# Router steps of a pair moved two pairs on, with norms, low parts, context loads and expert choices reordered around them

## The chip, the cores and the metric

The kernel runs on one core of a Trainium2 chip. The metric is the device time of one launch in microseconds (us), taken as the median of a few runs. The engines are called PE (TensorE), DVE (VectorE), ACT (ScalarE), POOL (GpSimd) and SP (SyncE, which here only issues DMAs). Each runs its own list of instructions in order and waits on semaphores for the others.

## What is computed

Sixteen batches of 128 rows of width 256 go through cross attention with 16 heads and then through a feed-forward layer with one shared expert and twelve routed experts, of which each row takes its best two:

```
x = x + attention(layernorm(x), ctx, ctx, masks)          # 16 heads of 16
n = layernorm(x)
logits = (n @ Wr + br) / 1.5                               # 12 experts
top_val, top_idx = top_k(logits, 2);  w = softmax(top_val)
x = x + geglu(n @ Ws1 + bs1) @ Ws2 + bs2 + sum_k w_k * expert[top_idx_k](n)
```

All matrix products keep about fp32 accuracy: an operand is split into a high part and a low part (fp32r), and three products are added up.

## The kernel before

**Stages.** The first third of the time is attention, worked in eight pairs of batches (PAIRS = 8, two batches each, pair p holds batches 2p and 2p+1). Then the rows are scattered by expert into a DRAM table by indirect DMAs on POOL (`scatter`, L1913), half of the shared expert is computed meanwhile, and 43 tiles of 128 rows go through the routed experts (from about 263 us to the end, matmuls L790 and L823). At the end the rows are gathered back.

**One pair on PE** (`pair`, L664; the order is written out by hand). PE works on three things interleaved: the attention of pair p, the projections of the next pair (steps "k", "q", "v", called by `put`), and the transposes of the normalised x of the pair after it (step "xT"). For a batch it computes the scores of all 16 heads into the four banks of ps_s (`scores`, L563: a mask product, L568, then 24 matmuls, L574), transposes the probabilities in four groups (`prob_transposes`, L585), multiplies them by the values (`values`, L595) and transposes the result (`out_transposes`, L603). The scores of a batch can be written only when DVE has taken those of the batch before.

**DVE in a pair** (`pair`, L1451). The scores of a batch are two units: unit 4p and 4p+1 for batch 2p, 4p+2 and 4p+3 for batch 2p+1. Each takes a `softmax_max` (L1317) and a `softmax_add` (L1324), and ACT then takes the exponential in place. `softmax_add` of a unit waits until PE has transposed the two groups of the unit two before it, since they share a buffer. Between them DVE makes the low parts of k, q and xT, the statistics of the first layer norm (`ln1_stats`, L1218), the division by the softmax sum (`norm`, L1334), the residual with the statistics of the second layer norm (`residual`, L1344), and xn2p, the second layer norm of a finished pair (`ln2_apply`, L1359).

**The router** of a pair has two steps: "r" transposes xn2p on PE (L488), ACT copies it out (xn2T, L997), and "l" multiplies by Wr (L539), DVE adds the bias into logits (L1283). In pair p the kernel before makes the router of pair p-1, near the end of the pair, directly behind `ln2_apply(p-1)`.

**Banks.** The steps of all pairs share two PSUM banks in turn. `order(p)` (L314) lists the steps of a pair, `base_of(p)` (L324) is the number of its first one, and a step's number decides its bank. The semaphore xb_free counts the steps whose bank is free again; step n on PE waits until step n-2 is free.

**Choices.** When the logits of batches 0 to 7 are there, DVE picks the best two experts (`choose(0, 0)`, `choose(1, 0)`, L1406), PE counts the ranks (step "n", in pair 6), and `row_numbers(0)` (L1428) makes the table rows and releases rows_ready, which POOL waits for before its first scatter. Batches 8 to 11 and 12 to 15 follow later in the same way.

**POOL in a pair** (the loop under `normalise_x(2)`): the first norm of pair p+2 (`normalise_x`, L1843), the scale of the second norm of pair p-1 (`rstd`, L1798), the split of the context of pair p+2 (`split_ctx`, L1833), and a share of the conversion of the shared expert's weights. **SP in a pair** (L429): load the context, save xn2p, zero an eighth of the scatter table (`fill`, L415, 3.3 MB each, eight of them). All eight fills must have landed before the first scatter.

Of the kernel before, what the change touches and what calls it, by code (L numbers as in the profile page):

```python
# [18 lines left out]
B, S, D = 16, 128, 256  # L19
# [33 lines left out]
def build(nc, x_d, ctx_d, pad_d, sub_d, wq_d, wk_d, wv_d, bias_d, bst_d, tab_d, ws1_d, ws2_d, w1_d,  # L53
# [260 lines left out]
    def order(p, first, last):  # L314

        if last:
            return ["r", "l", "n"]
        if first:
            return ["xT", "k", "q", "v", "xT"]
        if isinstance(p, int) and p == PAIRS - 2:  # L320
            return ["k", "q", "n", "v", "r", "l"]
        return ["k", "q", "v", "xT", "r", "l"]

    def base_of(p, first):  # L324

        return len(FIRST) if first else 6 * p + len(FIRST) - 1
# [15 lines left out]
    def each_pair(eng, body):  # L342

        body(0, 0, True, False)
        with eng.Fori(0, (PAIRS - 4) // 2) as i:
            body(i * 2 + 1, 1, False, False)
            body(i * 2 + 2, 0, False, False)
        body(PAIRS - 3, 1, False, False)
# [25 lines left out]
    with block:  # L374
# [3 lines left out]
        def _(sp):  # L378
# [61 lines left out]
            sp.wait_ge(c_split, PAIRS - 1)  # L440
            load_ctx(PAIRS - 1)
# [41 lines left out]
        def _(pe):  # L483
# [180 lines left out]
            def pair(p, par, first, last):  # L664
# [5 lines left out]
                def put(s, parts=(0, 1), again=False):  # L670
# [6 lines left out]
                    elif s in ("r", "l"):  # L677
                        router(s, p - 1, idx, bank, index_of("r", p, first, last) + 1)
# [17 lines left out]
                else:  # L696
                    prev = p * 2 - 1
                    prob_transposes(prev, 0)
                    put("k", (0,))
                    prob_transposes(prev, 1)  # L700
# [11 lines left out]
                    put("n")  # L712
# [238 lines left out]
        def _(sc):  # L951
# [82 lines left out]
            def pair(p, par, first, last):  # L1034
# [5 lines left out]
                def put(s, again=False):  # L1040
# [4 lines left out]
                    if s == "r":  # L1045
                        router(s, idx, bank)
# [9 lines left out]
                else:  # L1056
                    prev = p * 2 - 1
                    prob_copy(prev, 0)
# [4 lines left out]
                    exp(p * 4, 0)  # L1063
                    out_copy(prev)
                    put("q")
# [6 lines left out]
                put("xT", first)  # L1072
                prob_copy(cur, 3)
                put("r")
# [4 lines left out]
                exp(p * 4 + 3, 3)  # L1079

# [127 lines left out]
        def _(ve):  # L1208
# [242 lines left out]
            def pair(p, par, first, last):  # L1451
# [5 lines left out]
                def put(s, again=False):  # L1457
# [6 lines left out]
                    elif s in ("r", "l"):  # L1464
                        router(s, p - 1, idx, bank)
# [13 lines left out]
                else:  # L1479
# [606 lines left out]
```

## Time and profile before

| | us |
|---|---|
| median of 3 runs (643.98 to 647.44) | 644.26 |
| profiled execution, its own time | 646.02 |
| its span | 644.2 |
| PE busy / DVE / POOL / ACT | 582.1 / 447.1 / 364.5 / 282.6 |

PE is busy for 90% of the span. The chain of work that ended last runs for 72% of the span over PE, 12% over DVE and 5% over POOL. In the line of the page that shows PE's granted clock in 40 slices of 16 us, the last two thirds are at nine tenths or more throughout, while the attention stage goes up and down:

```profile
PEclk9799879789799989799999999999999999999998
```

### The profile page before, as it was taken

What the parts mean: (1) busy time and instruction counts of PE and PEld (TensorE: products, weight loads), DVE (VectorE), ACT (ScalarE), POOL (GpSimd) and SP (SyncE); (2) the same over time, 40 slices, a digit from 0 to 9 for tenths busy, and PEclk for the clock granted to TensorE, in tenths of its full rate; (3) what the DMA queues carried; (4) which work ended last, traced back from release to release, by engine and by line L of the source; (5) the groups of instructions that cost most, each with busy time, mean ns of one, the idle gap of its engine ahead of it and who ended that gap; (6) DMA issues with size and microseconds to landing.
All of it is one profiled execution on the core that took longest, in us unless ns stands there. A gap on an engine that the chain in (4) does not pass through costs nothing.

```text
span 644.2 us, 14068 instructions
## 1 busy us (share of the span) xinstructions
PE 582.1 (90%) x4092; PEld 479.8 (74%) x4093; DVE 447.1 (69%) x976; ACT 282.6 (44%) x629; POOL 364.5 (57%) x419
## 2 busy tenths in 40 slices
PE   7597979879788778799999999999999999999995
PEld 6465757656556777587887888878887888889995
DVE  5588668577678867667766677766676776665767
ACT  3255536454356623344444444444444444444432
POOL 3533151452108878699983886778886684000773
PEclk9799879789799989799999999999999999999998
DMA  9940651628651432364535365263465241110443
GB/s 289 395 173 31 216 185 61 244 99 292 227 214 68 172 140 91 122 225 156 204 136 179 95 222 188 81 228 130 144 222 183 86 131 33 33 34 18 139 134 121
DMA packets 47620, 98.91 MB, mean 154 GB/s; under 512 B 4449, under 2 KB 23521, under 8 KB 47585
## 3 DMA queue, kind: packets, MB, share of 16 engines
q1 hardware_dynamic: 36192, 50.41, 22.5%
q0 software_dynamic: 10976, 47.72, 22.2%
q10 hardware_dynamic: 416, 0.33, 0.2%
q8 instruction: 21, 0.34, 0.2%
q14 instruction: 15, 0.11, 0.1%
HBM read 57.15 MB, written 39.19 MB: 150 GB/s over the span
## 4 chain that ended last, share of the span: by engine, by line
PE 72%; DVE 12%; issue 5%; POOL 5%; ACT 3%; SPq 2%; DMA 1%; DVEq 0%; ACTq 0%; POOLq 0%
PE ps_s L790 29%; PE ps_o L823 9%; PE ps_o L824 5%; PE ps_s L752 4%; PE ps_t L800 3%; PE ps_t L585 3%; PE ps_s L568 2%; POOL rows_in L1913 2%; PE ps_s L574 2%; DVE prob L1324 2%; PE ps_x L510 2%; PE ps_t L510 2%; DVE nmax L1317 1%; PE ps_s L800 1%; PE ps_x L539 1%
## 5 line engine op out<-in xcount | busy, mean ns | idle before, releaser
L790 PE MATMUL ps_s<-ring,xTh 128*128 (+1 forms) x516 | 153.4, 419 | 0.5 <-DVE xTl L1638 0.5
L790 PEld LDWEIGHTS ps_s<-ring,xTh 128*128 128x128 f32 x516 | 89.2, 191 | 14.6 <-DVE xTl L1638 0.8
L1624 DVE TENSOR_TENSOR ag<-ps_s,up_bias 128x512 f32<-128x512 f32 x129 | 89.1, 691 | 12.1 <-PE ps_s L790 7.4
L823 PE MATMUL ps_o<-ring,hTh 128*128 x258 | 96.0, 410 | 0.8 <-issue 0.8
L1814 POOL TENSOR_TENSOR ring<-stage,ring 128x512 fp32r<-128x512 f32 x76 | 95.7, 1292 | 1.1
L790 PE MATMUL ps_s<-ring,xTl 128*128 (+1 forms) x258 | 81.0, 395 | 0.0
L824 PE MATMUL ps_o<-ring,hTl 128*128 x258 | 72.3, 280 | 0.0
L1800 POOL TENSOR_TENSOR ve<-mv,eps 128x2 f32<-128x2 f32 x16 | 3.5, 216 | 116.9 <-DVE mv L1356 100.6
L2025 POOL DMA_INDIRECT gath<-rows_out,idx_out x32 | 31.0, 968 | 65.8 <-DMA rows_out<-y_row 56.3
L1629 DVE TENSOR_TENSOR ag<-ag,ps_s 128x256 f32<-128x256 f32 x129 | 54.3, 421 | 16.0 <-ACT ps_s L1105 0.5
L1105 ACT ACTIVATE ps_s<-ag 128x256 f32<-128x256 f32 x129 | 50.2, 389 | 32.4 <-DVE ag L1624 31.0
L980 ACT ACTIVATE probT<-ps_t 128x512 f32<-128x512 f32 x64 | 37.8, 597 | 52.4 <-PE ps_t L585 51.2
L790 PEld LDWEIGHTS ps_s<-ring,xTl 128*128 128x128 f32 x258 | 48.8, 189 | 11.4
L1113 ACT ACTIVATE hTh<-ps_t 128x256 fp32r<-128x256 f32 x86 | 33.1, 385 | 53.6 <-PE ps_t L800 53.6
L1647 DVE TENSOR_TENSOR y_row<-ps_o,y_lo 128x256 f32<-128x256 f32 x43 | 18.3, 425 | 55.0 <-ACT y_lo L1128 55.0
L823 PEld LDWEIGHTS ps_o<-ring,hTh 128*128 128x128 f32 x258 | 48.5, 188 | 10.6 <-issue 1.0
L1827 POOL TENSOR_TENSOR ring<-stage,ring 128x512 fp32r<-128x512 f32 x40 | 51.0, 1300 | 1.2
L1633 DVE TENSOR_TENSOR hTl<-ps_t,hTh 128x256 fp32r<-128x256 f32 x86 | 36.1, 420 | 21.5 <-issue 16.8
L824 PEld LDWEIGHTS ps_o<-ring,hTl 128*128 128x128 f32 x258 | 48.9, 189 | 0.0
L1324 DVE TENSOR_TENSOR prob<-ps_s,nmax 128x1024 f32<-128x1024 f32 x32 | 39.1, 1221 | 13.2 <-PE ps_t L585 12.9
L752 PE MATMUL ps_s<-xgh,ring 128*128 128x256 f32 x256 | 47.4, 292 | 0.3
L1317 DVE TENSOR_REDUCE nmax<-ps_s 128x8 f32<-128x1024 f32 x32 | 38.9, 1217 | 10.3 <-PE ps_s L574 8.7
(254 smaller groups left out, 1290.1 us busy)
## 6 DMA issues: line engine op xcount, KB each, us to landing
rows_in<-y_row SPq DMA_DIRECT2D x8, 3328.0 KB, 13.7
stage<-in_w POOLq DMA_DIRECT2D x12, 1536.0 KB
stage<-in_w POOLq DMA_DIRECT2D x12, 768.0 KB, 5.4
up_bias<-in_bias POOLq DMA_DIRECT2D x12, 768.0 KB, 5.1
xrow<-rows_in SPq DMA_DIRECT2D x43, 128.0 KB, 2.2
rows_out<-y_row SPq DMA_DIRECT2D x43, 128.0 KB, 1.8
c_raw<-in_ctx SPq DMA_DIRECT2D x8, 256.0 KB, 10.7
xn_all<-xn2p SPq DMA_DIRECT2D x8, 256.0 KB, 2.6
```

Of the source, the lines that this page charges most:

```text
L752: last = pe_.matmul(ps_s[:, c, half * D:(half + 1) * D], weights(place, off + k * 2 * HS + half * D + col, P), x[:, k, :], start=n == 0, s ...
L790: last = pe_.matmul(ps_s[:, i, :], x[:, c, :], weights(place, off + c * 2 * HR + i * 2 * D, 2 * D), start=n == 0, stop=n == 5)
L823: pe_.matmul(ps_o[:, :], hTh[i][:, c, :], weights(place, a, 2 * D), start=i == 0 and c == 0, stop=False)
L824: pe_.matmul(ps_o[:, 0:D], hTl[i][:, c, :], weights(place, a, D), start=False, stop=False)
L980: act.activation(probT[:, g, :, :], ps_t[:, bank, :].rearrange("p (j t) -> p j t", j=4), ACT.Identity).then_inc(pt_copied, 1)
L1105: act.activation(ps_s[:, i, D:2 * D], ag[i][:, 1, :], ACT.Gelu).then_inc(gelu_done[i], 1)
L1317: vec.tensor_reduce(nmax[:, :, :], group_scores(n), AX.X, ALU.max, negate=True).then_inc(maxed, 1)
L1324: vec.tensor_tensor(prob[n % 2][:, :, :, :].rearrange("p a j t -> p j a t"), src, nmax[:, :, :].rearrange("p j (a o) -> p j a o", o=1).bro ...
L1624: vec.tensor_tensor(ag[i][:, :, :].rearrange("p a n -> p (a n)"), ps_s[:, i, :], bias, ALU.add)\
L1629: vec.tensor_tensor(ag[i][:, 0, :], ag[i][:, 0, :], ps_s[:, i, D:2 * D], ALU.mult).then_inc(hid_done[i], 1)
L1814: last = pool.tensor_tensor(lo_ap[:, c:c + PIECE], src[:, c:c + PIECE], hi_ap[:, c:c + PIECE].bitcast(f32), ALU.subtract)
L1827: last = pool.tensor_tensor(both[:, c:c + 2, 1, :], raw[:, c:c + 2, :], both[:, c:c + 2, 0, :].bitcast(f32), ALU.subtract)
```

## The change

The steps are reordered; the arithmetic stays the same.

- **PE.** In pairs 2 to 6 the router is that of pair p-2, whose xn2p was made in the pair before, and it stands at the beginning: "r" first of all, "l" behind the first half of "k". Pair 6 makes the router of pair 5 as well, at its end ("R" and "L"), with three filler matmuls (`spin`) between them. Step "xT" moves behind the third group of values, and the rank step "n" in pair 6 moves from the middle to behind `out_transposes(cur)`. Pairs 0 and 1 make no router.
- **ACT.** "q" is copied before `out_copy(prev)`, "xT" after `out_copy(cur)`.
- **DVE.** "l" goes ahead of the first `softmax_add`, "k" ahead of the second; `ln1_stats` is for pair p+2 in place of p+3; `ln2_apply` moves behind `softmax_add(4p+3)`, "xT" after it. `choose(0, 0)` moves from pair 5 to pair 6, `choose(1, 0)` from the end of pair 5 to the middle of pair 6, "n" and `row_numbers(0)` to behind `ln2_apply`.
- **POOL.** `split_ctx` comes first, `normalise_x` and `rstd` last, and then a new wait for xn2_ready, that is until DVE has made xn2p.
- **SP.** xn2p is saved first, then the context is loaded (for pair p+3), then the table is filled.

```
--- before.py
+++ after.py
         if isinstance(p, int) and p == PAIRS - 2:
-            return ["k", "q", "n", "v", "r", "l"]
-        return ["k", "q", "v", "xT", "r", "l"]
+            return ["r", "l", "k", "q", "v", "n", "R", "L"]
+        return ["r", "l", "k", "q", "v", "xT"]
...
             def pair(p, first):
-                sp.wait_ge(c_split, p + 2)
-                load_ctx(p + 2)
-                if not first:
+                if first:
+                    sp.wait_ge(c_split, 2)
+                    load_ctx(2)
+                    fill(1)
+                    sp.wait_ge(c_split, 3)
+                    load_ctx(3)
+                else:
                     save_xn2(p - 1)
-                fill(p + 1)
+                    sp.wait_ge(c_split, p + 3)
+                    load_ctx(p + 3)
+                    fill(p + 1)
...   (PE)
                     prev = p * 2 - 1
+                    put("r")
                     prob_transposes(prev, 0)
                     put("k", (0,))
+                    put("l")
                     prob_transposes(prev, 1)
...
                     out_transposes(prev)
-                    put("n")
...
                 values(0, par, cur, (1,))
-                put("xT", again=first)
                 prob_transposes(cur, 3)
                 values(0, par, cur, (2,))
-                put("r")
+                put("xT", again=first)
                 values(0, par, cur, (3,))
-                put("l")
                 out_transposes(cur)
+                put("n")
                 next_scores()
+                if "R" in todo:
+                    put("R")
+                    pe.wait_ge(xb_free, index_of("L", p, first, last) - 1)
+                    spin(3, step_bank[bank_of("L", p, first, last)][:, 0:D])
+                    put("L")
...   (DVE)
                 else:
+                    put("l")
                     softmax_add(p * 4, 0)
-                    softmax_shift(p * 4 + 1, 1, p * 2)
+                    softmax_max(p * 4 + 1, 1, p * 2)
                     put("k")
-                    if isinstance(p, int) and p == PAIRS - 3:
+                    softmax_add(p * 4 + 1, 1)
...
+                    if isinstance(p, int) and p == PAIRS - 2:
                         choose(0, 0)
-                    elif not isinstance(p, int):
-                        ln1_stats(p + 3)
+                    else:
+                        ln1_stats(p + 2)
+                    put("q")
                     softmax_max(p * 4 + 2, 2, p * 2 + 1)
                     norm(p - 1, 1)
-                    put("q")
+                if isinstance(p, int) and p == PAIRS - 2:
+                    choose(1, 0)
                 softmax_add(p * 4 + 2, 2)
                 if not first:
                     residual(p - 1, 1)
+                softmax_max(p * 4 + 3, 3, p * 2 + 1)
+                softmax_add(p * 4 + 3, 3)
+                if not first:
+                    ln2_apply(p - 1)
+                put("xT", first)
                 if isinstance(p, int) and p == PAIRS - 2:
                     put("n")
                     ve.wait_ge(xb_free, index_of("n", p, first, last) + 1)
                     row_numbers(0)
-                softmax_max(p * 4 + 3, 3, p * 2 + 1)
-                if not first:
-                    ln2_apply(p - 1)
-                softmax_add(p * 4 + 3, 3)
-                put("xT", first)
                 norm(p, 0)
                 residual(p, 0)
-                if first:
-                    ve.wait_ge(x_rest_in, 16)
-                    ve.wait_ge(router_in, 32)
-                    ln1_stats(3)
-                put("l")
                 softmax_max(p * 4 + 4, 0, p * 2 + 2)
-                if isinstance(p, int) and p == PAIRS - 3:
-                    choose(1, 0)
+                put("L")
...   (POOL)
             for p in range(1, PAIRS - 1):
                 if p + 2 < PAIRS:
-                    normalise_x(p + 2)
-                rstd(ln2_var, ln2_rs, mv2, ve2, rs2, p - 1, pstep2)
-                if p + 2 < PAIRS:
                     split_ctx(p + 2)
...
+                if p + 2 < PAIRS:
+                    normalise_x(p + 2)
+                rstd(ln2_var, ln2_rs, mv2, ve2, rs2, p - 1, pstep2)
+                gp.wait_ge(xn2_ready, p)
```

## Rows read from the trace of the kernel before

**Rows 1.** Windows by pair (pairs 1, 2, 6): window, length, busy times, PE clock, DMA.

```profile
44.10:69.89 25.79, 22.36 (x223) 16.43 (x219) 18.80 (x38) 12.90 (x20) 11.77 (x16) 0.87 0.28 101
69.89:95.88 25.99, 22.55 (x223) 16.54 (x219) 18.15 (x33) 12.90 (x20) 8.55 (x10) 0.89 0.44 156
...
174.74:199.45 24.71, 20.16 (x226) 14.84 (x223) 18.31 (x41) 12.39 (x19) 5.26 (x7) 0.99 0.56 207
```

**Rows 2.** Windows within pair 2, the long first part and the end.

```profile
69.89:85.50 15.61, 15.58 (x170) 11.65 (x166) 12.89 (x24) 9.63 (x16) 1.09 (x3) 1.00 0.27 89
85.50:95.88 10.38, 6.97 (x54) 4.89 (x53) 5.26 (x10) 3.26 (x5) 7.47 (x8) 0.72 0.71 258
```

**Rows 3.** Timeline of PE, end of pair 2: start, duration, engine, line, [idle before].

```profile
87.56 0.63 PE L488 MATMUL ps_t<-const,xn2p 128*128 128x128 f32 x4 [2.06 <-DVE xn2p L1364]
...
89.89 1.82 PE L539 MATMUL ps_x<-wr,xn2T 128*128 128x12 f32 x8 [1.35 <-ACT xn2T L997]
```

**Rows 4.** Timeline of PE, end of pair 6.

```profile
192.60 0.70 PE L585 MATMUL ps_t<-const,prob 128*128 128x128 f32 x4 [1.70 <-ACT probT L980]
...
194.77 0.63 PE L488 MATMUL ps_t<-const,xn2p 128*128 128x128 f32 x4 [1.12 <-DVE xn2p L1364]
...
196.09 1.06 PE L539 MATMUL ps_x<-wr,xn2T 128*128 128x12 f32 x8 [0.33 <-ACT xn2T L997]
197.00 0.64 PE L603 MATMUL ps_o<-const,outT 128*128 128x128 f32 x4
```

**Rows 5.** Windows, the same work in pair 6 and in pair 2.

```profile
194.77:199.45 4.68, 4.31 (x52) 2.99 (x53) 2.60 (x7) 2.98 (x4) 3.46 (x5) 1.00 0.42 153
87.56:95.88 8.32, 6.97 (x53) 4.86 (x53) 3.20 (x8) 2.97 (x4) 5.49 (x6) 0.65 0.88 320
```

**Rows 6.** Timeline of PE, pair 2 and the end of pair 0.

```profile
71.31 0.66 PE L585 MATMUL ps_t<-const,prob 128*128 128x128 f32 x4
...
77.51 1.04 PE L568 MATMUL ps_s<-mask_b,ident_b 128*128 x4
...
79.39 0.66 PE L603 MATMUL ps_o<-const,outT 128*128 128x128 f32 x4
...
84.50 0.64 PE L585 MATMUL ps_t<-const,prob 128*128 128x128 f32 x4
```

```profile
41.74 0.66 PE L603 MATMUL ps_o<-const,outT 128*128 128x128 f32 x4 [0.78 <-ACT outT L985]
```

**Rows 7.** Timeline of ACT, the copy of xn2T in pair 2.

```profile
89.24 0.60 ACT L997 ACTIVATE xn2T<-ps_t 128x512 f32<-128x512 f32 x1 [3.45 <-DVE xTl L1268]
```

**Rows 8.** Window of DVE in pair 2: length, busy, PE clock; and its low part of k.

```profile
75.88:85.40 9.52, 9.17 (x20) 1.00 0.01 2
```

```profile
77.02 1.40 DVE L1275 SCALAR_TENSOR_TENSOR km_lo<-ps_t,const,km_hi 128x512 fp32r<-128x512 f32 x2
```

**Rows 9.** Timeline of DVE: xn2p in pairs 2 and 6, choice in pair 5, row numbers.

```profile
85.46 1.96 DVE L1364 TENSOR_SCALAR xn2p<-x_all,mv,rs 128x256 f32 x2
...
156.42 0.20 DVE L1380 TENSOR_SCALAR lg<-logits 128x96 f32<-128x96 f32 x1
...
158.40 1.22 DVE L1317 TENSOR_REDUCE nmax<-ps_s 128x8 f32<-128x1024 f32 x1
...
191.05 0.23 DVE L1413 TENSOR_TENSOR pos<-ps_t,const 128x96 f32<-128x96 f32 x1
...
192.68 0.17 DVE L1422 CAST idx_top<-best 128x8 int32<-128x8 f32 x1
...
193.90 0.73 DVE L1364 TENSOR_SCALAR xn2p<-x_all,mv,rs 128x256 f32<-128x256 f32 x2
```

**Rows 10.** Timeline of POOL: the norm of x in pair 2, first scatter, last rstd.

```profile
90.80 2.43 POOL L1850 TENSOR_SCALAR xn<-x_all,mv,rs 128x256 f32<-128x256 f32 x2
...
193.86 1.12 POOL L1913 DMA_INDIRECT rows_in<-xn_all,idx_top  x1 [1.69 <-PE ps_t L585]
...
225.20 0.72 POOL L1802 TENSOR_TENSOR rs<-ve,half 128x2 f32<-128x2 f32 x1
```

**Rows 11.** Timeline of PE, the wait for the last pair's xn2p.

```profile
226.84 1.09 PE L488 MATMUL ps_t<-const,xn2p 128*128 128x128 f32 x4 [3.46 <-DVE xn2p L1364]
```

**Rows 12.** The last two table fills: timeline of SP, and their time to landing.

```profile
166.82 2.98 SPq L417 DMA_DIRECT2D rows_in<-y_row  x2
```

```profile
DMA to landing us min/median/max: 10.9/15.7/20.5
```

More of the change, by code:

```diff
@@ L319, in order @@
             return ["xT", "k", "q", "v", "xT"]
+        if isinstance(p, int) and p == 1:
+            return ["k", "q", "v", "xT"]
         if isinstance(p, int) and p == PAIRS - 2:
-            return ["k", "q", "n", "v", "r", "l"]
-        return ["k", "q", "v", "xT", "r", "l"]
+            return ["r", "l", "k", "q", "v", "n", "R", "L"]
+        return ["r", "l", "k", "q", "v", "xT"]
     def base_of(p, first):
-        return len(FIRST) if first else 6 * p + len(FIRST) - 1
+        if first:
+            return len(FIRST)
+        if isinstance(p, int) and p in (1, PAIRS - 1):
+            return len(FIRST) + 5 if p == 1 else base_of(PAIRS - 2, False) + 8
+        return 6 * p + len(FIRST) - 3
     def index_of(s, p, first, last, again=False):
@@ L344, in each_pair @@
         body(0, 0, True, False)
+        body(1, 1, False, False)
         with eng.Fori(0, (PAIRS - 4) // 2) as i:
-            body(i * 2 + 1, 1, False, False)
             body(i * 2 + 2, 0, False, False)
-        body(PAIRS - 3, 1, False, False)
+            body(i * 2 + 3, 1, False, False)
         body(PAIRS - 2, 0, False, False)
@@ L429, in pair @@
             def pair(p, first):
-                sp.wait_ge(c_split, p + 2)
-                load_ctx(p + 2)
-                if not first:
+                if first:
+                    sp.wait_ge(c_split, 2)
[4 more added lines that the diff above has]
+                else:
                     save_xn2(p - 1)
-                fill(p + 1)
+                    sp.wait_ge(c_split, p + 3)
+                    load_ctx(p + 3)
+                    fill(p + 1)
             pair(0, True)
@@ L677, in put @@
                     elif s in ("r", "l"):
-                        router(s, p - 1, idx, bank, index_of("r", p, first, last) + 1)
+                        router(s, p - 2, idx, bank, index_of("r", p, first, last) + 1)
+                    elif s in ("R", "L"):
+                        router(s.lower(), p - 1, idx, bank, index_of("R", p, first, last) + 1)
                     else:
@@ L1044, in put @@
                     idx, bank = index_of(s, p, first, last, again), bank_of(s, p, first, last, again)
-                    if s == "r":
-                        router(s, idx, bank)
+                    if s in ("r", "R"):
+                        router("r", idx, bank)
                     else:
@@ L1057, in pair @@
                     prev = p * 2 - 1
+                    put("r")
                     prob_copy(prev, 0)
@@ L1463, in put @@
                         rank_step(idx, bank, batch_in(p))
-                    elif s in ("r", "l"):
-                        router(s, p - 1, idx, bank)
+                    elif s in ("l", "L"):
+                        router("l", p - (2 if s == "l" else 1), idx, bank)
                     else:
@@ L1492, in pair @@
                     residual(p - 1, 1)
+                softmax_max(p * 4 + 3, 3, p * 2 + 1)
+                softmax_add(p * 4 + 3, 3)
+                if not first:
+                    ln2_apply(p - 1)
+                put("xT", first)
                 if isinstance(p, int) and p == PAIRS - 2:
```

10 lines of the change are left out of this document (5 added, 5 removed).

## Prediction

> **What bounds the kernel now.** I read the chain of work that ended last, then windows of one pair each, then the timelines of PE, DVE, ACT and POOL through pair 2, and at last POOL from 190 to 230 us. The change touches only pairs 0 to 6, so what counts is what sets their pace and what hands the gain on.
>
> A pair takes 25.8 to 26.0 us in the ordinary case, DVE is busy for 18.2 us of it and PE for 22.6 [rows 1], so no engine is full. The windows within pair 2 show where the loss is: for 15.6 us PE works without a gap at a clock of 1.00, then come 10.4 us with 7.0 us of work at a clock of 0.72 [rows 2]. That end begins with two stalls: 2.06 us for xn2p from DVE, and 1.35 us for its copy by ACT [rows 3]. After them PE works at its lower level (1.2 GHz). The same work, from the router's transposes to the end of the pair, takes 8.32 us there and 4.68 us in pair 6 [rows 5]; the stalls in those windows are 1.35 and 0.33 us [rows 3, 4], so the low clock costs 8.32 - 1.35 - (4.68 - 0.33) = 2.6 us. Per pair the router's place costs 2.06 + 1.35 + 2.6 = 6.0 us. Pairs 1 to 5 show this pattern.
>
> Behind attention stands POOL. From the first scatter at 193.86 to the second norm's scale of the last pair at 225.20 it works through its list with gaps of 0.3 us [rows 10], and PE then waits 3.46 us for the norm made from it [rows 11]. So the expert stage starts when POOL is through, and POOL starts on rows_ready, which DVE gives at 192.85, the end of row_numbers(0) [rows 9]; the scatter follows 1.0 us later. The row's releaser names PE, but I take the row numbers, which end closer.
>
> **The steady pair after.** I mark the end of the second group of transposes of the old batch as T; there DVE may start the first softmax_add. In pair 2 before, T is 71.31 + 0.66 = 71.97 [rows 6], 2.08 us behind the pair's start.
>
> From T to the scores of the next pair, PE: the fourth group of transposes of the current batch starts at T + 12.5 (84.50) [rows 6]. It stays there though xT no longer stands ahead of it, since the copy of the third group had ended only just before it. Three steps at high clock follow. By the gaps between starts, 0.35 to 0.6 us each, the group of values is through at T + 13.4, xT at T + 13.9, the last values at T + 14.3. Then PE waits for out_copy: 0.72 us, taken as in pair 0, where the same order gave 0.78 [rows 6]. outT takes 0.5, so the next scores start at T + 15.5. (Starts of about equal spacing on PE are my estimate from the row of the pattern; the sum of the three is 1.8.)
>
> From the scores to the next T: scores 79.39 - 77.51 = 1.88 [rows 6]; r 0.49 and first transposes 0.41. The copy of xn2T takes 0.60 [rows 7], starts when r ends, and k waits for its bank through it: 0.4 us of stall, where 0 and 1.35 [rows 3] are the bounds. Half of k 1.0, l 197.00 - 196.09 = 0.91 [rows 4], second transposes 0.6. Together 5.7 us. The period is 15.5 + 5.7 = **21.3 us** against 26.0.
>
> Does another engine take the bound? DVE's add of the second unit must be through before the scores at T + 5.5. It now has the low part of k ahead of it: add and max to T + 2.55, the low part 1.40 [rows 8] to T + 4.1, the transposes it waits for end at about T + 3.9, add to T + 5.35. That is 0.2 us ahead, the thinnest cover of all. The third unit's chain is as before. The last add ends at T + 14.6, 0.9 us before PE can use it, because ln2_apply no longer stands in front of it. ACT's exponentials end 0.6 us before the copy of xn2T is due. POOL makes the norm of x just in time now: statistics end at T + 6.5, its three instructions with the 2.43 us one [rows 10] take 3.5 us, and xT needs it at T + 13.4. The context is split a whole pair ahead of its use, and the load for it now goes ahead of the 3.3 MB fill. So these moves cost nothing; if POOL's norm came 4 us later it would stop PE at xT.
>
> The new POOL wait holds nothing of use: behind it in the queue are split_ctx and the weight conversion, needed a pair later or more, and POOL is busy 5 to 12 us of a pair [rows 1]. What it gives is shown by xn2p: 1.96 us while POOL works, 0.73 us while POOL is idle [rows 9]. The Trainium skill (GPSIMD Engine Reference, Specifications) says that GpSimd shares its SBUF interfaces with VectorE and contends with some of its modes; the trace agrees. Without the wait the apply would cost 1.2 us more, which matters only in pair 6, ahead of the row numbers: the sum below would be 20.2 in place of 21.4.
>
> **Up to pair 6.** Pair 1 has no router. T there is 44.10 + 2.08 = 46.2 in both kernels. After: T of pair 2 is 46.2 + 21.3 = 67.5, of pair 6 152.6 (four more periods). Before, pair 6 starts at 174.74 [rows 1], so T is 176.8 to 177.1. The gain there is **24.4 us**. The statistics removed from pair 0 were hidden.
>
> **Pair 6** takes both choices in. DVE from the low part of k at T + 2.7: in pair 2 the stretch from the second add to the last max, with that low part, is 9.17 us busy [rows 8]. Take off 1.0 for the statistics, add twice 158.40 - 156.42 = 1.98 for the choices, the last add 1.2, xn2p 0.73, and 192.85 - 191.05 = 1.8 for positions and row numbers [rows 9]: 9.2 - 1.0 + 4.0 + 1.2 + 0.7 + 1.8 = 15.9. So rows_ready comes at T + 18.7 or so = 171.4, and the first scatter at 172.4. Before it was at 193.86: **21.4 us** earlier. The rest of pair 6 on PE: L waits for nothing late, but DVE takes its logits only after norm, residual and max, at T + 22, and pair 7 waits for that. It starts at 174.6 in place of 199.45, 24.8 us earlier. As that is more than POOL's 21.4, POOL's unbroken list remains the later one, and PE's wait of 3.46 us grows to about 7. Three microseconds of the gain end there. The filler matmuls lie in a wait and cost nothing.
>
> The scatters also need the zeroed table. The last two fills were issued at 166.82 and needed up to 20.5 us [rows 12]. They now go out behind xn2p of pair 4, at T of pair 5 (131.3) + 15.5 = 147, and land at 168, 3 us ahead of rows_ready. Should they need 27 us, the gain shrinks by 3.
>
> The expert stage behind is bound by PE and by its own transfers, and shifts as a whole. **Sum:** the profiled execution's own 646.02 - 21.4 = 624.6. Its time stands 1.8 us above the median, so against 644.26 I predict **623.0**.
>
> **The rivals.**
> - *The clock falls all the same (0.08).* PE keeps two or three stalls of 0.4 to 0.7 us a pair. Against it: in pair 6 before, stalls of 1.70, 1.12 and 0.33 us [rows 4] left the clock at 0.99 [rows 1]. Price: 2.6 us in each of five pairs, 13 us: 636. The Trainium skill (TensorE: Matmul & The Clock Gate, A second HAM failure mode: psum-queue depth-cycling) tells of a kernel whose clock swung through frequent small idle spells between groups of matmuls; by that rule the time would be this rival's.
> - *The softmax loop becomes the bound (0.14).* r, l and the copy now stand between the scores and the transposes that free the buffer: DVE's first add of a pair comes 1.8 us later behind the scores than before. If the 0.2 us cover of the second add fails and waits add up to 1 to 2.5 us a pair, the period is 22.3 to 23.8 and the gain 21.4 - 5 to 12 = 9 to 16: 628 to 635. For it speaks that all covers are read to tenths.
> - *POOL's chain is shorter than I think (0.08):* full gain of 24.8, 619.5.
> - *Slower (0.02).* The low clock takes the whole pair. PE has 21.3 - 1.2 = 20.1 us of work in a pair after; at the low level the router's matmuls take 1.82 for 1.06 [rows 3, 4], 1.7 times. A pair would take 35 us, 9 more than now, and five of them make 46 us: 690. It becomes a loss once over 6.7 us of PE's work in a pair run low (4.7 / 0.7), where before 4.4 us did.
> - *It doesn't do what it says (0.02):* some wait ties r to the same pair after all, and the time stays at 644. Against it: xn2p of p-2 is made before the last scores of the pair before.
> - *The fills or the tail take some (0.06):* 626 to 629.
>
> **How the numbers follow.** The forecast, 619 to 627, has 0.60. The range takes in all of the softmax rival and the shorter chain and ends short of the falling clock: 616 to 635. Within 0.5% (about what a measurement of this kernel can tell from no change) is 641 to 647.5. Faster 0.96, same 0.02, slower 0.02.
>
> **What would show it.** Right: pairs 2 to 5 are 21 to 22 us long at a clock of 0.95 or more; PE has no wait for xn2p in them and one under 0.8 us for outT; xn2p takes 0.73 us; the first scatter is at 172 to 173; PE's wait for the last xn2p is 6 to 7 us. Wrong: a clock under 0.9 in a pair, PE waiting for DVE's probabilities at the scores, the first scatter held by the fills, or a part of the gain missing between 226 us and the end of the old trace.

## The result and the profile after

The changed kernel takes 627.0 us (median of 4 runs, 624.81 to 628.13) against 645.85 us (median of 4, 643.98 to 647.59): a ratio of 0.9705, with a 95% interval of 0.9659 to 0.975. The gain is 19 us where 21.4 were forecast. Of the 4.0 us between 623.0 and 627.0, 1.7 is the level of the kernel before, whose median of three runs was the base of the forecast (0.9705 x 644.26 = 625.3), and 2.3 is gain that didn't come. The profiled execution has a span of 625.5 us and a time of 627.47 us, so its own gain is 646.02 - 627.47 = 18.55 us.

First the pace. A window goes from the end of one pair's first-batch transposes of outT to the next (pairs 2 to 5). Columns: window, its length and PE's busy time, PE clock, DMA share, GB/s. It answers [rows 1]:

```profile
core 0: us, PE busy (x), PEclk, DMA share, GB/s
64.09:85.52 21.43, 19.86 (x219) 1.00 0.50 185
85.52:106.86 21.34, 19.85 (x219) 1.00 0.50 187
106.86:128.28 21.42, 19.86 (x219) 1.00 0.81 294
128.28:149.62 21.34, 19.86 (x219) 1.00 0.50 184
```

All four are within 0.1 us of 21.4, PE at full clock throughout, where [rows 1] had about 26 us at 0.87 to 0.89. PE's timeline of pair 2 shows what waits are left, in place of the 2.06 and 1.35 us of [rows 3]:

```profile
67.30 0.50 PE L520 MATMUL ps_t<-cTh,wkh 128*128 128x256 f32 x2 [0.42 <-ACT xn2T L1014]
...
82.19 0.66 PE L595 MATMUL ps_t<-const,prob 128*128 128x128 f32 x4 [0.41 <-ACT probT L997]
...
84.86 0.66 PE L613 MATMUL ps_o<-const,outT 128*128 128x128 f32 x4 [0.72 <-ACT outT L1002]
```

Three waits of 0.4 to 0.7 us, and none for xn2p. DVE makes xn2p of pair 5, in pair 6, in 0.72 us (before, 0.73 at this place and 1.96 in pair 2 [rows 9]), and the row numbers follow at once:

```profile
170.86 0.72 DVE L1382 TENSOR_SCALAR xn2p<-x_all,mv,rs 128x256 f32<-128x256 f32 x2
...
173.15 0.17 DVE L1440 CAST idx_top<-best 128x8 int32<-128x8 f32 x1
```

Then POOL's list, to be laid beside [rows 10]: first scatter 193.86 - 174.36 = 19.5 us earlier, last scale 225.20 - 205.67 = 19.53 us earlier. The first row names the save of xn2p as its releaser, but the scatter follows the end of the row numbers (173.32) by 1.0 us, as before. The third row is the bias load ahead of the expert loop; the kernel before had it at 263.48, so 1.0 us of the gain has gone by then (18.54).

```profile
174.36 1.12 POOL L1932 DMA_INDIRECT rows_in<-xn_all,idx_top  x1 [4.68 <-DMA xn_all<-xn2p]
...
205.67 0.72 POOL L1821 TENSOR_TENSOR rs<-ve,half 128x2 f32<-128x2 f32 x1
...
244.94 0.57 POOL L1977 DMA_DIRECT2D up_bias<-in_bias  x1 [6.85 <-DVE idx_out L1552]
```

Last the end of attention on PE and DVE, with [rows 11]. Pair 7 starts 199.45 - 176.12 = 23.3 us earlier, but PE's wait for the last xn2p is 3.50 us, as before (3.46), and not 7:

```profile
176.12 1.09 PE L595 MATMUL ps_t<-const,prob 128*128 128x128 f32 x8 [0.43 <-DVE logits L1301]
...
189.93 0.66 PE L595 MATMUL ps_t<-const,prob 128*128 128x128 f32 x4 [1.77 <-ACT prob L1006]
...
207.31 1.09 PE L498 MATMUL ps_t<-const,xn2p 128*128 128x128 f32 x4 [3.50 <-DVE xn2p L1382]
```

```profile
182.29 2.79 DVE L1366 TENSOR_TENSOR x_all<-x_all,att 128x256 f32<-128x256 f32 x1
...
192.81 1.69 DVE L1382 TENSOR_SCALAR xn2p<-x_all,mv,rs 128x256 f32<-128x256 f32 x2 [1.44 <-POOL rs L1821]
```

DVE's residual add took 2.79 us (0.88 at its place before, 0.42 in the ordinary case), and DVE then stood 1.44 us for POOL's scale of pair 6. Both stand beside one stretch of POOL's timeline: from 181.86 on it converts the first expert's weights, and the scale of pair 6 comes at 192.06, ahead of the conversion's last piece. That is 17.7 us behind the first scatter, as before (211.55 - 193.86).

```profile
181.86 3.69 POOL L1827 TENSOR_SCALAR ring<-stage 128x512 fp32r<-128x512 f32 x6
185.63 6.20 POOL L1833 TENSOR_TENSOR ring<-stage,ring 128x512 fp32r<-128x512 f32 x5
```

The missing gain, by stretch of this execution:

| stretch | forecast | seen | lost |
|---|---|---|---|
| T of pair 1 (start and pair 0) | 46.2 | 48.2 | 2.0 |
| five periods | 5 x 21.3 | 5 x 21.38 | 0.4 |
| T of pair 6 to the first scatter | 19.7 | 19.3 | -0.4 |
| first scatter to the end | 0 | 19.5 - 18.55 | 1.0 |

The sum is 3.0, against 21.4 - 18.55 = 2.85. The first line needs a second look, since the change hardly touches that stretch. The scores of pair 0's second batch ran at the low clock: the mask product took 1.74 us (1.04 in the kernel before), and from its start to the first transposes it was 3.25 us in place of 1.88 (34.51 - 32.63), which is 1.4 us of the 2.0:

```profile
32.92 1.74 PE L578 MATMUL ps_s<-mask_b,ident_b 128*128 128x512 bf16 x4 [2.15 <-DVE prob L1342]
...
43.74 0.65 PE L613 MATMUL ps_o<-const,outT 128*128 128x128 f32 x4 [0.78 <-ACT outT L1002]
```

Compare the second row with 41.74 in [rows 6]. The experiments below repeat it.

### The profile page after: what moved, and what is told of

Read it like the earlier page. It is cut to its first block, busy times and chain, and to the rows that moved or that the text cites. A ratio compares the mean times of both kernels' runs of the same rounds, so it can differ in the third digit from the quotient of the medians.

```text
span 625.5 us, 14081 instructions
## 1 busy us (share of the span) xinstructions
PE 573.8 (92%) x4098; PEld 474.6 (76%) x4099; DVE 443.2 (71%) x976; ACT 281.9 (45%) x629; POOL 364.3 (58%) x419
## 4 chain that ended last, share of the span: by engine, by line
PE 77%; DVE 8%; POOL 5%; issue 4%; ACT 4%; SPq 2%; DMA 1%; ACTq 0%; DVEq 0%; POOLq 0%
PE ps_s L807 30%; PE ps_o L840 10%; PE ps_o L841 5%; PE ps_s L769 4%; PE ps_t L595 3%; PE ps_t L817 3%; PE ps_o L605 2%; PE ps_s L578 2%; POOL rows_in L1932 2%; PE ps_s L584 2%; PE ps_t L520 2%; PE ps_t L532 2%; PE ps_s L817 2%; PE ps_x L828 1%; PE ps_x L520 1%
## 5 line engine op out<-in xcount | busy, mean ns | idle before, releaser
L595 PE MATMUL ps_t<-const,prob 128*128 128x128 f32 x256 | 39.4, 279 | 6.5 <-ACT probT L997 3.7
L1827 POOL TENSOR_SCALAR ring<-stage 128x512 fp32r<-128x512 f32 x76 | 44.9, 618 | 0.4
```

The lines of the kernel that those rows point to most:

```text
L595: last = pe_.transpose(ps_t[:, bank, j * P:(j + 1) * P], prob[g // 2][:, g % 2, j, :], ident)
L1827: last = pool.tensor_scalar(hi_ap[:, c:c + PIECE], src[:, c:c + PIECE], 1.0, 0.0, ALU.mult, ALU.add)
```

## The experiments

Twelve runs were made, in three groups of four, two of them of the changed kernel itself, each group on a chip of its own beside the kernel before. On the chip of the second group the kernel before took 647.27 us, on those of the first and third 675.18 and 676.14. Only kernels of one group are compared by their times. Where a difference from the changed kernel is wanted and the group did not hold it, the traces are compared.

**The low clock alone.** The kernel before, with filler matmuls where PE waited for xn2p and for xn2T in pairs 1 to 5:

```diff
-            def router(s, q, idx, bank, router_free=None):
+            def router(s, q, idx, bank, router_free=None, fill=0):
...
+                    spin(8 * fill, step_bank[bank][:, 0:D])
...
+                    if fill:
+                        pe.wait_ge(xb_free, idx - 1)
+                        spin(2, step_bank[bank][:, 0:D])
```

The first stands ahead of the wait for xn2p, the second ahead of the wait for xn2T.

> The kernel before, with the router where it was, but PE runs eight filler matmuls (about 2 us) into the router's own bank while it waits for xn2p in pairs 1 to 5, and two more while it waits for the copy of xn2T. Both stalls stay, only PE is not idle in them. Theory (stall and low clock are two separate costs of 3.4 and 2.6 us a pair): the clock stays over 0.95 in pairs 1 to 5, each becomes 2.4 to 2.6 us shorter, the time falls by 12 to 13 us, to about 98% of before. Rival (the gain of the change is the stall, and the low clock is covered by DVE's loop): the clock rises but the time falls by less than 4 us.

It took 666.12 us against 675.18, ratio 0.9882 (0.9837 to 0.9926): 9 us less, where 12 to 13 were expected. One of its windows, to be compared with the 26 us of [rows 1]:

```profile
67.40:91.51 24.11, 24.08 (x240) 1.00 0.47 166
```

The clock is 1.00, and a pair 24.1 us long though nothing was moved. PE has no gap left, since the fillers are longer than the waits they fill. In PE's timeline of that kernel they hold it from 84.66 to 88.21 and from 89.10 to 90.07, 4.5 us, where the waits were 3.4 [rows 3]:

```profile
84.66 3.72 PE L615 MATMUL ps_t<-y_row 128*128 128x256 f32 x16
88.21 0.60 PE L488 MATMUL ps_t<-const,xn2p 128*128 128x128 f32 x4
...
89.10 1.13 PE L615 MATMUL ps_x<-y_row 128*128 128x256 f32 x4
90.07 0.96 PE L543 MATMUL ps_x<-wr,xn2T 128*128 128x12 f32 x8
```

So the clock alone gives about 2 us a pair as it stands, and some 3 with fillers cut to fit (my estimate, 1.1 us less filler). The other 2.7 us a pair, from 24.1 to 21.4, needed the move. (The 26.0 us of the kernel before are from another chip; on this one only its time is known, and 9 us over five pairs are 1.8 each.) The forecast's split of 2.6 for the clock and 3.4 for waits was right in kind.

**POOL's new wait.** The changed kernel without the one line:

```diff
                 rstd(ln2_var, ln2_rs, mv2, ve2, rs2, p - 1, pstep2)
-                gp.wait_ge(xn2_ready, p)
```

> The changed kernel without POOL's wait for xn2_ready at the end of its loop. The prediction priced this at +1.2 us by the row numbers of pair 6. Looking again at POOL's list in pair 6 it has nothing left to do there, so I now expect: xn2p takes 1.9 us in pairs 2 to 5 and 0.73 us in pair 6, the last softmax_add is ahead of it and is not delayed, and the time stays within 0.3 us of the changed kernel. Rival (the prediction's): 1.2 us longer.

It took 650.95 us. Its pairs are those of the changed kernel, 21.43 and 21.36 us. DVE's timeline of pair 6, and POOL's of pair 3, say why:

```profile
169.91 0.73 DVE L1382 TENSOR_SCALAR xn2p<-x_all,mv,rs 128x256 f32<-128x256 f32 x2
```

```profile
87.86 0.62 POOL L1858 TENSOR_SCALAR cTh<-c_raw 128x512 fp32r<-128x512 f32 x1 [5.87 <-DMA c_raw<-in_ctx]
```

Without the wait xn2p takes 0.73 us as well, in pair 6 and in the pairs before it, where 1.9 was expected. POOL stands there all the same, for 5.87 us, since its next work is the split of a context that has not come: SP issues that load only behind the save of xn2p, and so only when xn2p is made. In the changed kernel POOL is idle from 83.0 to 88.8 us in the same way, and xn2p is made at 84.32. The wait neither gains nor costs, and the 1.2 us that the prediction gave it are not there.

**The place of ln2_apply.** The changed kernel with ln2_apply ahead of the last softmax_add, as in the kernel before. The expectation says that POOL's wait was kept, but the kernel that ran has it taken out too, so it is to be compared with the one above (650.95 us), from which only this order differs.

```diff
                 softmax_max(p * 4 + 3, 3, p * 2 + 1)
-                softmax_add(p * 4 + 3, 3)
                 if not first:
                     ln2_apply(p - 1)
+                softmax_add(p * 4 + 3, 3)
...
                 rstd(ln2_var, ln2_rs, mv2, ve2, rs2, p - 1, pstep2)
-                gp.wait_ge(xn2_ready, p)
```

> The changed kernel with ln2_apply put back ahead of the pair's last softmax_add on DVE, POOL's wait kept. Theory: with POOL idle xn2p takes 0.73 us, the last add ends at T + 15.3 where PE can start the scores at T + 15.5, so the period stays at 21.4 us and the time within 1 us of the changed kernel. Rival (the order of DVE's list is what took the stall away): each pair is 0.7 us or more longer, 4 us in all.

649.84 us, and pairs of 21.44 and 21.36 us: no difference. By the forecast's own reading the last add ends 0.9 us before PE can use it; 0.7 us of apply ahead of it fits in.

**POOL's last scale, first try.** The changed kernel with the scale of the last pair ahead of the scatters of tiles 5 to 7 (the kernels before and after have it ahead of tile 7 alone):

```diff
-            for t in range(3, 7):
+            for t in range(3, 5):
                 scatter(t)
             rstd(ln2_var, ln2_rs, mv2, ve2, rs2, PAIRS - 1, pstep2)
-            scatter(7)
+            for t in range(5, 8):
+                scatter(t)
```

> The changed kernel with POOL's rstd of the last pair moved ahead of three of the eight scatters of the tiles 3 to 7, which it followed. Theory (after attention POOL's list is the later one): PE's wait for the last xn2p falls from 3.5 us to under 1 us, and the time falls by 2 to 3 us. Rival (the tail is bound elsewhere, by DVE's tables and the gates of the shared expert): the wait goes, the time stays within 0.5 us.

652.6 us (651.53 to 654.1) beside 650.95 and 649.84 of the two above: no gain. On this chip that says little, since PE's wait for the last xn2p was only 0.81 and 0.46 us in those two and 0.27 us here. PE and DVE had already been held back in pair 7 (below, under the hardware), and POOL waited for DVE's statistics ahead of this scale, 4.36 us here and 3.63 in the kernel without POOL's wait: on this chip POOL's list is not the later one.

**Second group: the changed kernel again, both scales earlier, and two sizes of stall.**

> The changed kernel once more, to stand beside the three below on their own chip. Theory: its pairs 2 to 5 are 21.3 to 21.5 us long at a clock of 1.00 wherever it runs, since these pairs were the same to 0.1 us in three variants of it on another chip, and the pair-1 start differs only in steps of about 1 us (43.7, 42.7, 41.6 us for the first transposes of outT). Rival: the 2.0 us that pair 0 lost in its first trace belongs to the change, and the first transposes of outT stand at 43.7 again. A start at 41.6 to 42.7 speaks for run-to-run scatter.

626.91 us (624.11 to 627.93) against 647.27: ratio 0.9694 (0.967 to 0.9717), the first result again. The transposes of outT stand at 41.84 us this time, 0.1 us from the kernel before:

```profile
41.84 0.66 PE L613 MATMUL ps_o<-const,outT 128*128 128x128 f32 x4 [0.78 <-ACT outT L1002]
...
205.55 0.63 PE L498 MATMUL ps_t<-const,xn2p 128*128 128x128 f32 x4 [3.05 <-DVE xn2p L1382]
```

Over all twelve traces of the changed kernel and its variants this row lies between 41.20 and 43.93, at 42.5 in the mean; the kernel before and its filler version have 41.74 and 42.64. So the 2.0 us at the start are scatter between executions, nearly all of them, and no cost of the change. The gain on this chip is 20.4 us.

This trace also answers what became of PE's lead in pair 7. The slow residual add of the first trace isn't here, and the wait for the last xn2p is nearly the same (3.05 us):

```profile
180.40 0.47 DVE L1366 TENSOR_TENSOR x_all<-x_all,att 128x256 f32<-128x256 f32 x1
...
190.96 1.68 DVE L1382 TENSOR_SCALAR xn2p<-x_all,mv,rs 128x256 f32<-128x256 f32 x2 [3.80 <-POOL rs L1821]
```

```profile
192.79 0.63 PE L498 MATMUL ps_x<-const,xn2p 128*128 128x128 f32 x4 [2.98 <-DVE xn2p L1382]
```

DVE now stands 3.80 us for POOL's scale of pair 6. Add and wait together are 4.27 us here and 4.23 in the first trace (2.79 + 1.44): whatever the add takes, xn2p of pair 6 comes when POOL has made that scale.

Now the list of POOL with both scales earlier, that of the last pair as above and that of pair 6 one piece of the conversion earlier:

```diff
-                    if ahead_of_last and c + PIECE == n:
+                    if ahead_of_last and c + 2 * PIECE == n:
```

> The changed kernel with POOL's list reordered in the last pair: the second norm's scale of the last pair made after the scatters of tiles 3 and 4 and not after those of 3 to 6, and the scale of the pair before it one piece of the weight conversion earlier. Theory (POOL's list holds the last xn2p, PE waits 3.50 us for it): the last scale comes 203.1 in place of 205.7, PE's wait falls from 3.5 to about 1 us, and the time falls by 2 to 3 us against the changed kernel on the same chip. Rival (behind it POOL's unbroken list of scatters, the transfers or DVE's tables hold the expert stage): the wait falls but the time stays within 1 us of the changed kernel's.

623.31 us (621.44 to 624.13), 3.6 us under the changed kernel beside it; the ratio to the kernel before is 0.9625 (0.96 to 0.9651). POOL's last scale comes at 200.93 in place of 203.91, and PE's wait falls from 3.05 to 1.07 us:

```profile
204.02 0.63 PE L498 MATMUL ps_t<-const,xn2p 128*128 128x128 f32 x4 [1.07 <-DVE xn2p L1382]
```

The two profiled executions differ by only 0.8 us in span, with the start 1.1 us later in this one, so some 2 us can be pointed at in the traces, and the rest of the 3.6 can't. This is the fastest kernel of the study.

How much stall does the clock bear? In pairs 2 to 5 of the changed kernel, ACT was given idle activations of 128x256 ahead of its copy of xn2T, two in the one kernel and five in the other:

```diff
                     sc.wait_ge(xb_free, idx)
+                    for t in (hTh + hTl)[0:idle]:
+                        act.activation(t[:, :, :], const[:, 0:2 * P].rearrange("p (c n) -> p c n", c=2), ACT.Identity)
                     act.activation(xn2T[:, :, :], ps[:, :].rearrange("p (c n) -> p c n", c=KC), ACT.Identity)
```

> The changed kernel with two idle activations of 128x256 (about 0.4 us each by the gate's activations) ahead of ACT's copy of xn2T in pairs 2 to 5, so that PE's wait at the first half of k grows from 0.4 to about 1.2 us. Theory (the clock holds through stalls of this size): +0.8 us in each of four pairs, pairs 2 to 5 of 22.2 us at a clock of 1.00, +3 to +4 us in all. Rival (the clock stood just above its fall): the low level comes back behind this stall, pairs of 24 to 25 us, +12 to +14 us.

> The same with five idle activations: PE's wait at k grows by 2 us to about 2.4 us, more than either of the two stalls of the kernel before (2.06 and 1.35 us), but alone. Theory (a stall of that size is what brings the low level): the clock of pairs 2 to 5 falls under 0.95 and each is longer by the 2.0 us of stall and by 1.5 to 2.6 us of slow work behind it, +14 to +18 us in all. Rival (it takes both stalls together, or the work in between): the clock stays at 1.00, pairs of 23.4 us, +8 us.

With two, 629.32 us, 2.4 us more than the changed kernel (3 to 4 were expected). PE's wait at k is 1.02 us and the clock stays:

```profile
66.79 0.50 PE L520 MATMUL ps_t<-cTh,wkh 128*128 128x256 f32 x2 [1.02 <-ACT xn2T L1016]
```

```profile
62.97:85.01 22.04, 19.86 (x220) 1.00 0.49 180
```

Four pairs at +0.6 us are the 2.4 us; an activation cost 0.3 us, not 0.4. With five, 638.04 us, 11.1 us more:

```profile
68.03 0.50 PE L520 MATMUL ps_t<-cTh,wkh 128*128 128x256 f32 x2 [1.94 <-ACT xn2T L1016]
```

```profile
63.29:86.27 22.98, 19.88 (x220) 1.00 0.47 173
86.27:111.96 25.69, 22.71 (x219) 0.87 0.42 155
111.96:136.16 24.20, 21.14 (x219) 0.93 0.73 260
136.16:160.47 24.31, 21.33 (x219) 0.93 0.43 162
```

The same stall of 1.9 us leaves one pair at full clock and brings the low level in three. Over the four pairs 97.2 - 85.5 = 11.7 us come on top, 6.1 of them the stalls themselves (4 x 1.52) and 5.6 the slow matmuls behind them: PE is busy for 2.8, 1.3 and 1.5 us more in the three pairs that are hit (22.71, 21.14 and 21.33 against 19.88). One trace shows it. This is between the two expectations: one stall is enough, but neither each time nor for as long as after the two stalls of the kernel before.

**Third group: fillers, SP's order, and POOL's conversion.**

> The changed kernel a third time, as the measure for the three below on the same chip. Pairs 2 to 5 of 21.3 to 21.5 us at a clock of 1.00; on the chip of the first two traces a median of 626 to 628 us; PE's wait for the last xn2p 3.0 to 3.5 us.

651.31 us (648.24 to 654.39), ratio 0.9636 (0.9601 to 0.9671). Pairs of 21.44 and 21.36 us again; PE's wait for the last xn2p has gone on this chip, since POOL itself stands 3.67 us for DVE's statistics ahead of its last scale.

The three filler matmuls of pair 6 taken out:

```diff
                     pe.wait_ge(xb_free, index_of("L", p, first, last) - 1)
-                    spin(3, step_bank[bank_of("L", p, first, last)][:, 0:D])
                     put("L")
```

> The changed kernel without the three filler matmuls between the last pair's R and L of pair 6. By the prediction they lie in a wait and cost nothing: without them the time is the same within 1 us and the clock of pair 7 stays. Rival: they are what keeps the clock up while PE waits there, and without them the low level comes back in pair 7: its clock falls by 0.1 or more and up to 2.6 us are lost, seen only in part at the end, since POOL's list is the later one.

648.25 us (643.93 to 649.35), ratio 0.9574 (0.9542 to 0.9606). They cost nothing or, by up to 3 us, something: the two intervals just touch. The clock is another matter. PE goes through the waits without them, 0.78, 0.71 and 0.34 us within 4.0 us, at full clock, and falls to the low level behind them:

```profile
171.08:178.00 6.92, 5.04 (x58) 1.00 0.21 77
178.00:184.68 6.68, 5.20 (x53) 0.74 0.23 81
```

```profile
177.83 1.66 PE L595 MATMUL ps_t<-const,prob 128*128 128x128 f32 x8 [0.34 <-ACT probT L996]
```

The same transposes take 1.12 us in all eleven traces that have the fillers. So, as far as one trace without them can show it, the rival is right about the clock: the fillers hold it there. It is wrong about the time, in which no loss can be seen. Three longer waits, of 1.70, 1.12 and 0.33 us, had left the clock at 0.99 in pair 6 of the kernel before [rows 4], so the length of the waits alone doesn't tell what the clock will do.

SP's queue as in the kernel before, all else as in the changed kernel. The load that was left over stands behind the loop:

```diff
                     load_ctx(2)
                     fill(1)
-                    sp.wait_ge(c_split, 3)
-                    load_ctx(3)
                 else:
+                    sp.wait_ge(c_split, p + 2)
+                    load_ctx(p + 2)
                     save_xn2(p - 1)
-                    sp.wait_ge(c_split, p + 3)
-                    load_ctx(p + 3)
                     fill(p + 1)
...
+            sp.wait_ge(c_split, PAIRS - 1)
+            load_ctx(PAIRS - 1)
```

> The changed kernel with SP's queue in the order of the kernel before (the context load of a pair ahead of the saved norm, made one pair later). By the prediction the moved loads gain and cost nothing: the same time within 1 us, pairs of 21.3 to 21.5 us. Rival: POOL's split of the context, or its norm behind it, comes too late for xT or v in the shorter pair, and PE or ACT waits for it: 0.5 us or more in each of four pairs, over 2 us in all.

662.48 us (661.01 to 668.38), 11.2 us more than the changed kernel beside it. This was the surprise. The windows:

```profile
63.24:87.42 24.18, 20.25 (x219) 0.98 0.47 164
87.42:111.73 24.31, 21.69 (x220) 0.92 0.47 164
111.73:138.71 26.98, 22.20 (x220) 0.88 0.68 237
138.71:161.32 22.61, 21.12 (x219) 0.94 0.48 169
```

The cause can be followed through three timelines, SP's, POOL's and PE's:

```profile
63.64 0.59 SPq L423 DMA_DIRECT2D rows_in<-y_row  x1
64.79 0.39 SPq L386 DMA_DIRECT2D c_raw<-in_ctx  x1
```

```profile
76.56 0.62 POOL L1858 TENSOR_SCALAR cTh<-c_raw 128x512 fp32r<-128x512 f32 x1 [15.78 <-issue]
...
82.23 2.44 POOL L1869 TENSOR_SCALAR xn<-x_all,mv,rs 128x256 f32<-128x256 f32 x2
```

```profile
84.72 0.66 PE L498 MATMUL ps_x<-const,xn 128*128 128x128 f32 x4 [2.35 <-POOL xn L1869]
```

The load of 256 KB stands 1.2 us behind the fill of 3.3 MB and is there at 76.56, 11.8 us after its issue (median of its eight loads 10.7 us; 3.1 us in the changed kernel's trace). POOL's list is in order, so the norm of x, which doesn't need the load, waits too, and ends at 84.67 where the changed kernel has it at 79.44. PE stands 2.35, 1.14 and 3.21 us at xT in pairs 2 to 4, and the low clock comes back with it.

The load isn't issued later than in the changed kernel (64.79 against 64.54 us), it only stands behind the fill. In the kernel before it stands there too and takes as long (median 10.7 us), and it did no harm. There POOL made the norm first (64.89) and the split of the context behind it, 21.6 us after the load was issued at 63.70:

```profile
85.31 0.62 POOL L1839 TENSOR_SCALAR cTh<-c_raw 128x512 fp32r<-128x512 f32 x1
```

The changed kernel has the split ahead of the norm, 2.9 us after the issue (67.41). So it is SP's old order together with POOL's new one that costs 11.2 us. No run has both of them old in the shorter pair.

Last, POOL's conversion moved behind the scatters of tiles 3 and 4, with the scale of pair 6 ahead of it:

```diff
-            first_w1(lambda: rstd(ln2_var, ln2_rs, mv2, ve2, rs2, PAIRS - 2, pstep2))
-            for t in range(3, 7):
+            for t in range(3, 5):
                 scatter(t)
+            rstd(ln2_var, ln2_rs, mv2, ve2, rs2, PAIRS - 2, pstep2)
+            first_w1(None)
             rstd(ln2_var, ln2_rs, mv2, ve2, rs2, PAIRS - 1, pstep2)
-            scatter(7)
+            for t in range(5, 8):
+                scatter(t)
```

> The changed kernel with POOL's list of the last pair in another order: scatters of tiles 3 and 4, the scale of pair 6, then the first weight conversion, then the last pair's scale, then the scatters of tiles 5 to 7. Theory (POOL's conversion slows DVE's residual add from 0.42 to 2.79 us and holds xn2p of pair 6 by 1.44 us): the add beside scatters takes 0.4 to 0.5 us, xn2p comes without a wait, the last xn2p 4 to 5 us earlier than in the changed kernel, and the time falls by 4 to 6 us, below the kernel with both scales earlier (3.6 us under the changed kernel). Rival (the load of the second expert's weights, now issued 5 to 6 us later, or the scatters behind it hold the expert stage): the time is that of the kernel with both scales earlier or above it.

655.4 us (652.6 to 656.4), 4.1 us more than the changed kernel, though the intervals of the two ratios still overlap (0.9661 to 0.9717 against 0.9601 to 0.9671). The residual add takes 0.42 us now, as expected, with POOL idle beside it, but the conversion has only moved on: xn2p of pair 6 stands beside it and takes 2.29 us.

```profile
188.86 0.42 DVE L1366 TENSOR_TENSOR x_all<-x_all,att 128x256 f32<-128x256 f32 x1
...
196.41 2.29 DVE L1382 TENSOR_SCALAR xn2p<-x_all,mv,rs 128x256 f32<-128x256 f32 x2
```

The last xn2p was expected 4 to 5 us earlier and stands at 209.89, where the changed kernel beside it has it at 209.87. Both traces lose 7.4 us to gaps of ACT ahead of its copies of outT (below), and in both POOL waits for DVE ahead of its last scale. So moving two tiles' scatters behind that scale gains nothing here and makes POOL's list later: its first bias load comes at 226.18 in place of 221.11. Whether the order gains on a chip without such gaps stays open.

## Why the prediction was right or wrong

**What bounds the kernel: right.** The two waits for xn2p and xn2T and the low clock behind them were the loss. The filler version got the clock back with nothing moved, and the version with 1.9 us of stall brought the low level back in three pairs of four.

**The steady pair: right, to 0.1 us.** 21.38 against 21.3. The copy of xn2T stops k for 0.42 us (0.4 forecast), outT 0.72 (0.72), and the fourth group of transposes starts at T + 12.5 (T + 12.5). The thin cover of the second softmax_add held.

**The clock rival: out.** PE's small waits left the clock of pairs 2 to 5 at 1.00, and so did one of 1.02 us. The rule cited for it (the Trainium skill, TensorE: Matmul & The Clock Gate, A second HAM failure mode: psum-queue depth-cycling) does not show in pairs 2 to 5 at waits of 0.4 to 1.0 us: the clock stays at 1.00. A lower clock came with one wait of 1.9 us a pair, and in pair 6 without the fillers.

**"These moves cost nothing": right for the change as a whole, but an unpriced step.** The forecast noted that the load now goes ahead of the 3.3 MB fill, and that a norm 4 us later would stop PE at xT. It did not see that the change needs the one to escape the other: with POOL's split ahead of its norm, SP's old order costs 11.2 us, nearly half of the 24.8 us (676.14 - 651.31) that the change gains on that chip. The two edits are a pair; one alone can't be priced at nothing.

**POOL's wait: wrong.** The step "without the wait the apply would cost 1.2 us more" took the duration of xn2p from a pair in which POOL was at work [rows 9] and didn't ask what POOL does at the new place. It does nothing there, because the load of its next work is issued behind the save of xn2p.

**"The filler matmuls cost nothing": right for the time.** Left out, they brought the low level in one trace (0.74 for 6.7 us) and no loss of time. The forecast took them as idle ballast and had no clock at stake there.

**The hand-over in pair 6: right in size.** First scatter at T + 19.3, forecast T + 19.7. The fills didn't hold it: issued at 149.77, they needed at most 20.3 us.

**T of pair 1: the reading was right, its execution wasn't typical.** The 2.0 us are scatter.

**PE's wait for the last xn2p "grows to about 7": wrong.** It stayed at 3.5 us. PE led POOL by 3.8 us more at the start of pair 7 (23.3 against 19.5) and had lost that by its end. The step that failed is that PE meets POOL's list only at the last xn2p. POOL's scale of pair 6 stands in the same list, 17.7 us behind the first scatter. Before, DVE came to it without a wait; now it comes earlier and is held for it, in the first trace 1.44 us behind a slow residual add, in the second 3.80 us behind a fast one. The lead ends there: in the second trace PE waits 2.98 us for xn2p of pair 6 and 3.05 us for the last, 6.0 in all. The conclusion drawn from the step, that POOL's list is the later one, was right on the chip of the second group: both scales earlier gave 3.6 us.

**The stage behind "shifts as a whole": off by 1.0 us in the first trace.** DVE's steps beside POOL's second conversion grow, such as hTl at 232.76, 1.31 us (0.53 before). But the second trace doesn't show the loss: from the first scatter to the end of the span it has 449.8 us, the first trace 451.1 and the kernel before 450.3. So the 1.0 us may be scatter, and no experiment took it apart.

## What to carry to other kernels

When a wait and a low clock stand together, fill the wait first: a version with filler matmuls is a few lines and tells what the clock alone is worth. When an engine's list is reordered, go through every transfer that it waits for again: here a load behind a large transfer landed 8 us later than one ahead of it, which did no harm while its user stood at the end of the pair and stopped PE once it stood at the start. And once an engine's list is what ends last, put the small result that someone awaits ahead of the bulk.

## What the runs showed of the hardware

**POOL beside DVE.** The same add of two SBUF tiles took 0.42 us with POOL idle or scattering, and between 0.46 and 2.79 us beside POOL's conversion of the first weights. In two executions of the changed kernel it began 0.45 and 0.43 us behind the conversion's start, and took 0.47 and 2.79 us; in the two kernels with longer stalls it began 0.45 us behind it both times, and took 0.46 and 2.78 us. The Trainium skill (GPSIMD Engine Reference, Specifications) says that GpSimd shares its SBUF interfaces with VectorE and contends with DVE instructions in a 2-port perf mode or with two SBUF inputs. The traces agree for the add, which has two, and show that the price isn't fixed. xn2p, which reads one SBUF tile, grew as well, from 0.73 to between 1.29 and 2.66 us; in which mode it ran no trace shows.

**Gaps without a releaser.** On the chips of the first and third group ACT stopped for 1 to 15 us at several places in and behind pair 7, where the traces name no event of this core. In the changed kernel's third trace the view of waits has, for 170 to 255 us:

```profile
ACT ag L1108 <- remote: 12.7, 3, 9.3
...
ACT outT L1002 <- remote: 7.4, 2, 5.5
```

The stretch of pairs 2 to 5 is the same there to 0.1 us, and on the other two chips neither wait appears. The kernel before ran 29 us longer there as well. What these gaps are was not found out. They hold ACT, PE and DVE back in pair 7, and in these traces POOL waits 2.2 to 4.4 us for DVE ahead of its last scale. This fits with a repair of POOL's list gaining 3.6 us on one chip and nothing on another: what isn't the later one can't be won back.
